# Moving the split of the next head pair's weights in the last attention of a graph network block

## The reference, cut to what matters

```
h = einsum('td,erd->ter', xf, A) + ba            # 8 experts of rank 16
delta = (einsum('ter,eor->to', h * combine, Bm) + combine @ bb) * SCALING
qkv = xf @ Wqkv.T + bqkv + delta                 # 768 -> 3 * 768
q, k, v = ...                                    # 12 heads of 64
attn = softmax(q @ k.T * 64 ** -0.5)             # 1250 x 1250 for each head
out = attn @ v
return out @ Wproj.T + bproj
```

## Time and profile before

| | us |
|---|---|
| median of 3 runs | 2965.63 (2957.41 to 2967.86) |
| the profiled execution | 2959.68 |
| its span, first to last instruction | 2957.9 |
| the six pairs, by TensorE's first product of each to the end of the last | 2194.8 to 2871.0 |
| pairs 1 to 4, each | 112.9 to 113.2 |
| TensorE busy in the span | 2637.5 (89%) |
| VectorE, GpSimd, ScalarE busy | 1599.5, 1266.3, 778.0 |

### The profile page before, as it was taken

How to read it: one execution, slowest core, us unless ns; L and a number is a source line. 1 busy time by engine, 2 the same in 40 slices (tenths; PEclk the granted TensorE clock), 3 DMA queues, 4 the chain that set the end, 5 groups by cost and what they waited for, 6 DMA issues and landing times.

```text
span 2957.9 us, 68470 instructions
## 1 busy us (share of the span) xinstructions
PE 2637.5 (89%) x24343; PEld 2008.1 (68%) x24343; DVE 1599.5 (54%) x3130; ACT 778.0 (26%) x1111; POOL 1266.3 (43%) x1376
## 2 busy tenths in 40 slices
PE   5998999978998859999999788986959999999989
PEld 4787888847676647888885667664537666666665
DVE  6576666654446654333333345546776646646631
ACT  2111121201222212211130121320135355365350
POOL 1685211147777745300005677773005164264271
PEclk9999999999999969999999899997979899999999
DMA  5233333459888966433236988998110000000013
GB/s 165 91 126 103 120 123 121 132 200 313 309 299 311 312 201 193 156 121 104 94 99 211 320 283 306 320 314 280 42 38 2 22 22 1 22 22 1 22 49 94
DMA packets 103837, 448.79 MB, mean 152 GB/s; under 512 B 20725, under 2 KB 21048, under 8 KB 99381
## 3 DMA queue, kind: packets, MB, share of 16 engines
q0 software_dynamic: 60352, 283.01, 28.5%
q1 hardware_dynamic: 40661, 123.20, 13.1%
q10 hardware_dynamic: 2592, 39.32, 3.9%
HBM read 361.50 MB, written 83.92 MB: 151 GB/s over the span
## 4 chain that ended last, share of the span: by engine, by line
PE 58%; DVE 17%; issue 8%; POOL 5%; DVEq 5%; DMA 4%; ACT 2%; POOLq 0%; ACTq 0%; SPq 0%
PE PS L1796 26%; PE PS L1806 4%; PE PS L2091 3%; PE PS L2174 3%; PE PS L1895 2%; PE PS L2157 2%; PE PS L1998 2%; DVE NMC L1716 2%; PE PS L1927 2%; PE PS L2158 2%; POOL GATA L732 2%; DVE RCP L1441 2%; POOL PL L769 2%; POOL ROW L732 1%; DMA MSG<-msg_table,SKEY 1%
## 5 line engine op out<-in xcount | busy, mean ns | idle before, releaser
L1796 PE MATMUL PS<-WHL,XT 128*125 (+1 forms) x2880 | 488.7, 329 | 6.3 <-DVE WHL L1132 4.2
L1796 PE MATMUL PS<-WHL,HT 128*125 (+1 forms) x2880 | 476.8, 328 | 13.2 <-DVE HT L1285 10.7
L1796 PEld LDWEIGHTS PS<-WHL,HT 128*125 (+1 forms) x2880 | 394.7, 138 | 91.6 <-DVE HT L1285 12.5
L1796 PEld LDWEIGHTS PS<-WHL,XT 128*125 (+1 forms) x2880 | 391.7, 138 | 82.6 <-issue 4.7
L769 POOL TENSOR_TENSOR PL<-PF 125x500 bf16<-125x500 f32 (+1 forms) x306 | 291.9, 981 | 252.6 <-ACT PF L984 248.8
L732 POOL DMA_INDIRECT GATA<-msg_table,SKEY x324 | 312.4, 964 | 144.0 <-issue 90.6
L1219 DVE SCALAR_TENSOR_TENSOR MSG<-PS,MSG 125x768 f16<-125x768 f32 x160 | 153.1, 957 | 353.0 <-ACT MSG L808 351.1
L808 ACT ACTIVATE MSG<-PS 125x768 f16<-125x768 f32 x160 | 129.6, 810 | 795.8 <-PE PS L1796 785.4
L732 POOL DMA_INDIRECT ROW<-msg_table,SKEY x216 | 213.7, 990 | 92.8 <-issue 60.5
L984 ACT ACTIVATE PF<-PS,QK 125x500 f32<-125x500 f32 (+1 forms) x360 | 212.8, 608 | 103.0 <-PE PS L2158 102.8
L2174 PE MATMUL PS<-V,PF 125*125 125x129 bf16 x1200 | 194.6, 258 | 26.3 <-POOL PL L769 24.2
(11 more groups left out here) (327 smaller groups left out, 4905.5 us busy)
## 6 DMA issues: line engine op xcount, KB each, us to landing
msg_table<-MSG SPq DMA_DIRECT2D x160, 336.0 KB
WST<-in_wg_dram ACTq DMA_DIRECT2D x16, 2304.0 KB, 10.3
WST<-in_wf_dram SPq DMA_DIRECT2D x7, 1536.0 KB, 6.2
KROW<-key_rows POOLq DMA_DIRECT2D x54, 192.0 KB, 3.8
WST<-in_wm_dram SPq DMA_DIRECT2D x6, 1152.0 KB
msg_table<-MSG SPq DMA_DIRECT2D x160, 39.0 KB
GATA<-msg_table,SKEY POOLq DMA_INDIRECT x324
ROW<-msg_table,SKEY POOLq DMA_INDIRECT x216
```

The lines of the kernel that those rows point to most:

```text
L1796: ins = pe.matmul(PS[0:ROWS, b0 + h, 0:HALF], X[:, xp, k, bass.ts(t, ROWS)], panel_part(slot, wp, k, h), start=k == 0 and xp + wp == 0, st ...
```

## The change

The split of the next pair's panel moves from the middle of the second half into the first half, and its low halves move from VectorE to GpSimd.

- `FH` and `FL` get a second place and are indexed by the panel's number modulo 2; the pad tile `FILL` shrinks by as much.
- GpSimd runs `ffn_scales` right after `panel_top` at the start of a pair. The one scale in it that the current pair still uses (`XWINV`) becomes `product_scale` and stays between tiles 33 and 34 (`NEXT_SCALE = 34`).
- ScalarE runs `split_ranks` between k2 and q1 of the first half instead of ahead of tile 38.
- GpSimd then runs the new `panel_low`: three multiplications that scale the panel in place, then three subtractions. VectorE's form did both in one instruction each.
- VectorE no longer splits in the loop (only the first panel, ahead of it). `ON_DVE` has eleven tiles, so GpSimd makes 49 low halves of a pair where it made 51.
- The next load of `WST` follows `w_lo` as before, now behind `shift_rows` of the same turn on SyncE.

```diff
-        FH = sb(qctx, "FH", [128, 2, 3 * 128], f16)
+        FH = sb(qctx, "FH", [128, 2, 2, 3 * 128], f16)
...
-        SPLIT_AT = 38
-        ON_DVE = (7, 11, 17, 21, 27, 31, 37, 41, 57)
+        NEXT_SCALE = 34
+        ON_DVE = (7, 11, 17, 20, 22, 31, 37, 41, 47, 50, 52)
...
+            def panel_low(q):
+
+                g.wait_ge(S["w_hi"], q + 1)
+                g.sem_inc(S["tick"], 1)
+                slot = bass.ds(q % 2, 1)
+                g.tensor_scalar(WST[:, WM:WM + 3 * 128], WST[:, WM:WM + 3 * 128], RS[:, FSC], None, ALU.mult)
+                g.tensor_scalar(WST[:, 0:WM], WST[:, 0:WM], SC[:, WSCALE], None, ALU.mult)
+                g.drain()
+                g.tensor_scalar(WST[32:64, WM + 3 * 128:WF], WST[32:64, WM + 3 * 128:WF], RS[32:64, FSC], None, ALU.mult)
+                g.drain()
+                high = FH[:, slot].rearrange("p a k c -> p (a k c)")
+                g.tensor_tensor(FL[:, slot].rearrange("p a c -> p (a c)"), WST[:, WM:WM + 3 * 128], high[:, 0:3 * 128], ALU.subtract)
+                g.tensor_tensor(WHM[:, slot, 1, :].rearrange("p a c -> p (a c)"), WST[:, 0:WM], WHM[:, slot, 0, :].rearrange("p a c -> p (a c)"), ALU.subtract)
+                g.drain()
+                g.tensor_tensor(high[32:64, 3 * 128:6 * 128], WST[32:64, WM + 3 * 128:WF], high[32:64, 3 * 128:6 * 128], ALU.subtract)
+                g.drain()
+                g.sem_inc(S["w_lo"], 1)
...
             with g.Fori(0, PAIRS) as it:
                 panel_top(it + (W_FFN + 1))
+                ffn_scales()
+                panel_low(it + (W_FFN + 1))
                 for n_ in range(2 * 3 * RT):
...
-                    if n_ == SPLIT_AT - 4:
-                        ffn_scales()
+                    if n_ == NEXT_SCALE:
+                        product_scale()
...
                 for r in HIGHS:
+                    if r == "q1":
+                        split_ranks(it + (W_FFN + 1))
...
-                    if n_ == SPLIT_AT:
-                        split_ranks(it + (W_FFN + 1))
...
-                        if r == "O10":
-                            split_low(it + (W_FFN + 1), WHM, WM, ranks=True)
```

More of the change, by code:

```diff
@@ L140, in graph_and_attentions_kernel @@
         qctx = top.enter_context(ExitStack())
-        FH = sb(qctx, "FH", [128, 2, 3 * 128], f16)
+        FH = sb(qctx, "FH", [128, 2, 2, 3 * 128], f16)
         FL = sb(qctx, "FL", [128, 2, 3 * 128], f16)
         QS = sb(qctx, "QS", [128, 2, N], f16)
-        FILL = sb(qctx, "FILL", [128, KT * D - 6 * 128 - N], f32)
+        FILL = sb(qctx, "FILL", [128, KT * D - 9 * 128 - N], f32)
         ROWS4 = sb(top, "ROW", [128, 4, D], f32)
@@ L737, in ffn_scales @@
                 g.tensor_scalar(SCI[:, WSCALE], SCI[:, POW], -1.0, float((254 + TOP) << 23), ALU.mult, ALU.add)
-                g.tensor_scalar(SC[:, XWINV], SC[:, POW], RS[:, UP], 2.0 ** -TOP / X_SCALE, ALU.mult, ALU.mult)
                 g.drain()
@@ L744, in ffn_scales, with product_scale @@
                 g.sem_inc(S["w_scale"], 1)
+            def product_scale():
+                g.tensor_scalar(SC[:, XWINV], SC[:, POW], RS[:, UP], 2.0 ** -TOP / X_SCALE, ALU.mult, ALU.mult)
+                g.drain()
[13 more added lines that the diff above has]
+                g.tensor_tensor(high[32:64, 3 * 128:6 * 128], WST[32:64, WM + 3 * 128:WF], high[32:64, 3 * 128:6 * 128], ALU.subtract)
+                g.drain()
+                g.sem_inc(S["w_lo"], 1)
             panel_top(W_FFN)
@@ L791, in split_ranks @@
                 act.wait_ge(S["w_scale"], q + 1)
-                act.activation(FH[:].rearrange("p k c -> p (k c)"), WST[:, WM:WF], ACT.Copy, scale=RS[:, FSC])
+                act.activation(FH[:, bass.ds(q % 2, 1)].rearrange("p a k c -> p (a k c)"), WST[:, WM:WF], ACT.Copy, scale=RS[:, FSC])
                 split_high(q, W=WHM, cols=WM)
@@ L1030, in split_low @@
                 if ranks:
-                    v.scalar_tensor_tensor(FL[:, 0, :], WST[:, WM:WM + 3 * 128], RS[:, FSC], FH[:, 0, :], ALU.mult, ALU.subtract)
-                    v.scalar_tensor_tensor(FH[32:64, 1, :], WST[32:64, WM + 3 * 128:WF], RS[32:64, FSC], FH[32:64, 1, :], ALU.mult, ALU.subtract)
+                    v.scalar_tensor_tensor(FL[:, q % 2, :], WST[:, WM:WM + 3 * 128], RS[:, FSC], FH[:, q % 2, 0, :], ALU.mult, ALU.subtract)
+                    v.scalar_tensor_tensor(FH[32:64, q % 2, 1, :], WST[32:64, WM + 3 * 128:WF], RS[32:64, FSC], FH[32:64, q % 2, 1, :], ALU.mult, ALU.subtract)
                 v.scalar_tensor_tensor(W[:, bass.ds(q % 2, 1), 1, 0:cols].rearrange("p a c -> p (a c)"), WST[:, 0:cols], SC[:, WSCALE],
@@ L2078, in ranks @@
                     c = slice(x * 128, (x + 1) * 128)
-                    return ((FH[:, 0, c], LTH[:, 0, :]), (FH[:, 0, c], LTL[:]), (FL[:, 0, c], LTH[:, 0, :]), (FH[0:96, 1, c], LTH[0:96, 1, :]))
+                    return ((FH[:, slot, 0, c], LTH[:, 0, :]), (FH[:, slot, 0, c], LTL[:]), (FL[:, slot, c], LTH[:, 0, :]), (FH[0:96, slot, 1, c], LTH[0:96, 1, :]))
                 def keys_or_queries(nm, c, first, end):
```

## The result

| | before | after |
|---|---|---|
| median of 4 runs, us | 2961.52 (2956.89 to 2967.86) | 2933.29 (2920.92 to 2936.94) |
| ratio | | 0.9886, 95% interval 0.9862 to 0.9910 |
| the profiled execution, us | 2959.68 | 2920.92 |
| the six pairs, first product to last | 674.6 | 635.7 |
| of it six first halves / six second halves | 327.8 / 337.7 | 330.9 / 296.7 |

The kernel became faster by 28 us (1.1%). The predicted median was 2930.1, the measured one is 2933.3. The profiled execution lost 38.8 us and lies 12 us under its median; before, it lay 2 us under the median of these four runs. All of the 38.8 us is in the pairs: 41.0 in the second halves, 1.0 between them, less 3.1 that the first halves grew.

A forecast was written before the change was run, and what follows sets the result against it. TensorE was taken as the bound in both halves of a pair, by its work and by its interruptions. Savings of 48.0 us less 12.5 added give 35.5; 2965.6 - 35.5 = 2930.1 us, range 2906 to 2954.

The forecast's parts named there:

- tile 37 to 47: Ten tile steps of the second half: from 10.88 us down to 8.95, saving 1.93 us a pair.
- tile 47 to 59: Twelve tile steps of the second half: from 14.00 us to the 7.75 of tiles 17 to 29, saving 6.25.
- the last tiles: End of a pair, where no scores follow and GpSimd's low halves are awaited: 0.2 us a pair taken off the saving.
- `panel_low`'s six instructions: GpSimd's low halves in the first half: 16.3 us with drains, ended at 2350.5, 13 us before they could delay the pair.
- `score_scale`'s wait: First half: VectorE waits for GpSimd's running multiplication, 1.5 us a pair and 4.6 in pair 0.
- six first halves grow: Cost added on the path: 5 x 1.5 + 4.6 for `score_scale` and 0.4 for pair 0's late scales, 12.5 us.
- ten steps at 0.90 are 8.95: Floor for tiles 37 to 47: the exponentials' spacing from tile 47 to 48, taken for all ten steps.
- second halves near 49.7 us: Sign expected in the changed kernel's profile: each second half takes about 49.7 us, where it took 57.7.
- the slower rival: VectorE's `score_scale` waits for all six GpSimd instructions, 10.4 us, and the clock falls: 2994 us, chance 0.06.
- The clock at the ends of pairs: Full clock still lost at a pair's end, so q0 stays about as dear; counted as nothing, at most 2.4 us.
- the clock holds: Rival: full clock kept at the ends of pairs too, about 2 us more saved in each pair: 2918 us, chance 0.15.
- VectorE's wait loses the clock: Rival: `score_scale`'s wait pauses TensorE until its clock halves over the tops, 2 to 3 us a pair: 2945, chance 0.13.

The follow-up runs named there:

- r_after: The changed kernel run again with nothing changed, for the spread of its times: median 2934.0 us, ratio 0.9895 to the kernel before.
- e3: The changed kernel, but VectorE makes the panel's low halves at their old place and has the old nine tiles: 2956.1 us, ratio 0.9972 to before.
- e7: The changed kernel with fourteen tiles of low halves on VectorE in place of eleven: 2921.0 us, ratio 0.9837 to before.
- e4: The changed kernel with the old list of nine tiles on VectorE: 2933.4 us, ratio 0.9872 to before.
- e1: The changed kernel with `score_scale` moved to the start of the pair, before GpSimd's panel instructions: 2917.2 us, ratio 0.984 to before.
- e6: The changed kernel without `panel_low`; VectorE makes the low halves in the first half, right after `score_scale`: 2957.4 us, ratio 0.9962 to before.
- e2: The changed kernel with one tensor input of `score_scale`'s first instruction made a scalar operand, its place unchanged: 2917.5 us, one run.

## Why the prediction was right

| its term | predicted, us | measured |
|---|---|---|
| tile 37 to 47, saved in a pair | 1.93 | 0.92 (9.96 left) |
| tile 47 to 59, saved in a pair | 6.25 | 6.25 (7.75 left) |
| the last tiles, lost in a pair | 0.2 | 0.50 (1.86 for 1.36) |
| six second halves | 48.0 | 41.0 |
| `panel_low`'s six instructions | 16.3 | 15.7 |
| `score_scale`'s wait, pairs 1 to 5 / pair 0 | 1.5 / 4.6 | 0.77 / 3.35 |
| six first halves grow | 12.5 | 3.1 |
| sum for the profiled execution | 35.5 | 38.8 |

In r_after's profile of the same kernel the second halves are the same 296.7 us, but the first halves grew by 10.4 us, near the forecast 12.5, and the pairs lost 31.6 us in place of 38.9. So the forecast's 35.5 lies between two profiles of one kernel. The medians differ by 28.2 us, 7.3 less than forecast; that 2933.3 still lies so near 2930.1 owes 4.1 us to the kernel before, whose median came out at 2961.5 with one more run, and not at the 2965.6 that the sum started from.

**The second halves.** The mechanism was right: the pause, the fall of the clock behind it and ScalarE's delay at tile 37 are gone, and the clock is kept to the end of the pair. e3 shows what ScalarE's part is worth by itself (1.5 us), and by difference the rest (5.3); no run has the low halves moved alone. The step that failed is "ten steps at 0.90 are 8.95". That pace is one step's, tile 47 to 48, and not every step has it. The profile of before held the right floor: the same ten steps under head 0, tiles 7 to 17, took 9.99 us there, and 37 to 47 now takes 9.96. For 47 to 59 I had used the counterpart under head 0, and that one came out exact. In pairs 0, 3 and 4 there was a little more to save than in pair 1 (14.58, 14.17 and 14.27 us before). The sign "second halves near 49.7 us" was meant by the cut of the earlier trace rows, and by that cut pair 1's takes 50.8; that the other cut gives 49.4 is no hit. In the changed kernel six of the ten steps are 0.89 or 0.90 long; the others, 38 to 41, around the change to the next chunk of queries, take 1.03, 0.98 and 1.41, and 43 to 44 takes 1.18. GpSimd's rate is a part of it: in pair 1 TensorE stands idle for 0.30 us between 40 and 41 for a GpSimd low half (and 0.11 between 43 and 44 for nothing that the profile shows), and three more tiles on VectorE took 0.3 away up to tile 17 and 0.2 here (e7). For the rest of the 1.0 us TensorE is recorded as busy, and why was not tried. I had counted the two low halves fewer as worth nothing, and so they were (e4), but three more were not.

**The tail** was underestimated by 0.3 us. I took the last tiles' wait for GpSimd as nearly what it had been; but tile 57 went from VectorE back to GpSimd, which then makes the last six in a row.

**`panel_low`.** The prices per column from the graph stage held: 6.11 for 6.3, 4.55 for 4.9, and 0.91 for 1.0. It started 2.3 us earlier in the pair than I had it, since pair 1's q0 now ran at the full clock (3.97 us for 6.19). The panel's load cost nothing, as forecast: it is issued 1.4 us behind the row's move, which still takes 2.08 us (2.07).

**`score_scale`.** It waited for one instruction, and not for all six: the slower rival is out. By the Trainium skill (SBUF — State Buffer, Who interferes with whom) the engine that issues first holds the shared ports for its whole instruction, and the trace agrees: GpSimd's multiplication began first, and `score_scale` ended 0.43 to 0.44 us before its end in 6 of 6 pairs. Whether the drain behind the multiplication was needed for that, as I had argued from the earlier trace rows, is not shown, since no run leaves it out. The wait was half of what I took, as it reached the multiplication nearer to its end (1.36 us before it, where my working had 1.7) and was let in 0.59 us before that end, where I took 0.13 from the earlier trace rows.

**The clock at the ends of pairs** was counted as nothing, and this was the second size that was off, to the other side. The full clock was kept at three of five starts in one profile and at none in the other. A start at half the clock costs 1.7 us (55.48 against 53.80), as the fall is now over after 3.4 us and no longer lies across the boundary for 13.6. In sum pairs 1 to 5 have shorter first halves than before, 272.3 us for 274.4, although each holds the new wait: the wait costs 0.96 (e1), so the clock gave back 5 x 0.96 + 2.1 = 6.9 us in this profile. The two misses, 7.0 in the second halves and 9.4 in the first, cancelled but for 2.4, and the rest is the 1.0 between pairs. That they cancelled is luck: r_after's profile has the first of them without most of the second. It was the forecast's way, with the rival "the clock holds" true in part.

**VectorE's wait loses the clock**: not in pairs 1 to 5. In pair 0 it does, behind the 3.5 us:

```profile
2231.00:2234.40 3.40, 1.83 (x20) 1.32 (x21) 3.20 (x4) 0.00 (x0) 2.84 (x4) 0.99 0.00 0
2234.40:2237.80 3.40, 3.40 (x26) 2.49 (x24) 2.64 (x3) 0.00 (x0) 3.40 (x1) 0.50 0.00 0
```

Pair 0's first half grew by 5.15 us: 3.35 of the wait, and about 1.7 for this stretch. The scales that come late there cost nothing that can be seen.

## What to carry to other kernels

When a piece is moved off a busy stretch, take the floor for what is left from the same steps elsewhere in the profile, and not the shortest step times their number: the former was exact for twelve steps and would have been for the ten. An idle stretch of a slow engine is a better home for side work than a gap of a fast engine on the path (e6), but look for two-tensor instructions of VectorE that meet it; a scalar operand or an earlier place removed that meeting for nothing. And where the time depends on a clock that falls at boundaries, compare medians of several runs: two profiles of one kernel differed by 17 us.

## What the runs showed of the hardware

- Where VectorE's splitting instructions met GpSimd's low halves, both were longer: one low half of each pair took 3.33 us in place of 1.01 (before and e3, six of six pairs each), and VectorE's three took 1.05, 1.27 and 3.28 us in pair 1 before, and 0.62, 0.61 and 2.62 with GpSimd idle (e6).
- VectorE's two-tensor instruction was let in about 0.6 us before the end that the profile gives for GpSimd's multiplication, in all six pairs; with the second input as a scalar operand it didn't wait at all (0.21 us inside the same multiplication, e2).
- On 128 partitions of float32 GpSimd's scaling took 6.11 us for 2304 columns (2.65 ns each) and its subtraction of two tensors 4.55 (1.97): the one-tensor instruction is the slower one here.
- After equal ends of pairs TensorE's clock sometimes fell to 1.2 GHz and sometimes not. Pairs 2 and 3 of the changed kernel run the same instructions up to the pause of 1.22 us, and only pair 3 fell. In r_after both did.
- Ahead of pair 0 stand 18435 TensorE matmuls that no change touched. Pair 0's first product came between 2192.9 and 2213.3 us over the 14 profiles. This is larger than several of the effects studied here.
